# Loading each group's results at its own count of landed units, adding them two groups at a time on TensorE, and adding groups 0 and 1 on VectorE

## What is computed

```python
logits = jnp.einsum('bsd,de->bse', x, Wg)
P = jax.nn.softmax(logits, axis=-1)
_, topk_idx = jax.lax.top_k(P, K)                    # K = 2 of E = 8 experts
mask = jax.nn.one_hot(topk_idx, E, dtype=x.dtype).sum(-2)
P_norm = P * mask / ((P * mask).sum(axis=-1, keepdims=True) + EPS)
h = jax.nn.gelu(jnp.einsum('bsd,edf->ebsf', x, W1) + b1[:, None, None, :], approximate=False)
y_e = jnp.einsum('ebsf,efd->ebsd', h, W2) + b2[:, None, None, :]
g = _silu(jnp.einsum('ebsd,bse->bsd', y_e, P_norm))
x = x + s * g                                        # s: the second block's attention-like branch
```

## Time and profile before

| | |
|---|---|
| median of 3 runs | 446.04 us (444.91 to 446.62) |
| profiled execution: span from the first to the last instruction | 445.2 us |
| TensorE busy | 409.0 us, 92% of the span |
| VectorE busy | 284.5 us, 64% |
| ScalarE busy | 213.8 us, 48% |
| GpSimd busy | 155.7 us, 35% |

### The profile page before, as it was taken

One profiled execution on the slowest core, in us unless ns is written; L12 is line 12 of the kernel. 1 busy time (PEld: TensorE's weight loads), 2 busy tenths in 40 slices (PEclk: granted clock), 3 DMA queues, 4 the chain that ended last, 5 costly groups with the idle time before them and its releaser, 6 DMA issues. The chain is left out here.

```text
span 445.2 us, 9851 instructions
## 1 busy us (share of the span) xinstructions
PE 409.0 (92%) x2944; PEld 344.6 (77%) x2944; DVE 284.5 (64%) x1137; ACT 213.8 (48%) x525; POOL 155.7 (35%) x215
## 2 busy tenths in 40 slices
PE   7699989999999999999988999888999999999882
PEld 7579777878869779787767779777899999998630
DVE  4889889888887878878867657412233343433327
ACT  3364555565554545543424353333555555555412
POOL 6340015013233340443433011534454555455510
PEclk9999999999999999999999999999999999999998
DMA  7449411154064330131222223321222222222576
GB/s 181 123 114 166 57 40 42 50 170 135 13 192 122 81 79 25 47 83 53 75 54 61 66 51 80 101 80 54 68 71 67 78 71 71 61 77 68 169 275 193
DMA packets 64210, 40.80 MB, mean 92 GB/s; under 512 B 18340, under 2 KB 57128, under 8 KB 64168
## 3 DMA queue, kind: packets, MB, share of 16 engines
q1 hardware_dynamic: 59472, 31.27, 28.2%
q0 software_dynamic: 4352, 8.99, 6.1%
q10 hardware_dynamic: 344, 0.03, 0.1%
HBM read 21.78 MB, written 18.48 MB: 90 GB/s over the span
## 5 line engine op out<-in xcount | busy, mean ns | idle before, releaser
L694 POOL DMA_INDIRECT routed<-send,slot x64 | 64.5, 1008 | 129.1 <-DMA routed<-send,slot 57.5
L703 POOL DMA_INDIRECT results<-nat,y_to x72 | 69.8, 969 | 89.0 <-DVE nat L1638 65.4
L1029 PE MATMUL psA<-xuT,w_all 128*128 128x256 f32 x288 | 68.9, 381 | 3.5 <-ACT h1T L1239 3.2
L1239 ACT ACTIVATE h1T<-psA,b1T 128x256 f32<-128x256 f32 x144 | 63.1, 473 | 12.0 <-PE psB L1052 7.5
L1029 PEld LDWEIGHTS psA<-xuT,w_all 128*128 128x128 f32 x288 | 50.6, 190 | 11.5 <-issue 2.9
L1041 PE MATMUL psC<-w_all,h1T 128*128 128x128 f32 x464 | 56.7, 275 | 1.0 <-DVE nat L1622 1.0
L1610 DVE TENSOR_SCALAR xu<-ring 128x256 f32 (+1 forms) x38 | 11.2, 295 | 71.2 <-DMA ring<-routed 67.0
L1041 PEld LDWEIGHTS psC<-w_all,h1T 128*128 128x128 f32 x464 | 54.1, 192 | 1.3 <-ACT h1T L1239 1.1
L1230 ACT ACTIVATE xuT<-psB 128x256 f32<-128x256 f32 x37 | 14.2, 383 | 61.6 <-PE psB L1019 45.8
L843 PE MATMUL psB<-xnT,w_l 128*128 128x512 f32 x64 | 34.3, 618 | 0.0
L1170 ACT ACTIVATE hg0T<-psB,b1T 128x512 f32<-128x512 f32 x32 | 22.0, 688 | 22.9 <-PE psB L845 22.8
(11 more groups left out here) (289 smaller groups left out, 851.8 us busy)
## 6 DMA issues: line engine op xcount, KB each, us to landing
ring<-routed SPq DMA_DIRECT2D x38, 130.0 KB
inv<-inv_room SPq DMA_DIRECT2D x8, 512.0 KB
w_all<-results SPq DMA_DIRECT2D x15, 256.0 KB, 4.1
routed<-ring SPq DMA_DIRECT2D x24, 130.0 KB, 6.7
n_room<-nT SPq DMA_DIRECT2D x8, 256.0 KB
w_all<-in_L_ffn_W_dram SPq DMA_DIRECT2D x1, 2048.0 KB
out_dram<-x_all SPq DMA_DIRECT2D x8, 256.0 KB, 2.3
results<-nat,y_to POOLq DMA_INDIRECT x72
```

What stands on the lines that cost most here:

```text
L694: pool.indirect_dma_start(routed[:, :], bass.IndirectOffsetOnAxis(ap=slot[par][:, c, t:t + 1], axis=0), send[par][:, c, t, :], None).then_ ...
L703: pool.indirect_dma_start(results[:, :], bass.IndirectOffsetOnAxis(ap=y_to[:, par, a:a + 1], axis=0), yw[:, par, a, :], None).then_inc(S[f ...
L1029: last = mm(psA[:, j // 2, (j % 2) * UNIT:(j % 2 + 1) * UNIT], w1_all[:, e, j * P:(j + 1) * P], xuT[:, :], start=True, stop=True)
L1239: f(h1T[:, j, :], psA[:, j // 2, (j % 2) * UNIT:(j % 2 + 1) * UNIT], ACT.Gelu, bias=b1T[:, n:n + 1]).then_inc(S["gelu_ready"], 1)
```

## The change

Four things change together.

1. **Counts per group.** VectorE now keeps how far each expert's region was filled after each group (`filled` has a row for each group), and `make_table()` works out two counts for each group from it: the number of units that must have landed before the group's lower rows are whole (that of expert 6), and the same for its higher rows (that of expert 7). SP reads these counts from `table` (`units_due`) and waits for each before it loads that group's rows.
2. **When a landing is told.** POOL waits for the unit ahead, and raises `y_landed`, between a unit's two transfers instead of behind them, and once more at the end.
3. **The sums.** VectorE adds the rows of groups 0 and 1 itself, from SBUF; TensorE takes the others two groups at a time: lower, lower, higher, higher.
4. **The surplus unit.** When the count of units is odd, POOL sends one unit too many. VectorE's part in that (`surplus_results`) now stands behind `finish(1)`, and gives it row numbers outside of the results.

```diff
-            def load_results(c, to, signal):
-                for g in range(groups):
-                    at = c * tokens + g * GW
-                    sp.dma_start(to[g], results[at:at + GW, :].rearrange("(p t) d -> p t d", t=TILES)
-                                 ).then_inc(signal[g], 16)
-
+        DUE_AT = 2 * E + 2
+        def units_due(eng, g, part):
+            at = DUE_AT + 2 * g + part
+            return eng.value_load(table[0:1, at:at + 1], min_val=FIRST_ALL, max_val=MAX_UNITS)
...
+            def load_results(c, g, to, signal):
+                at = c * tokens + g * GW
+                sp.dma_start(to[g], results[at:at + GW, :].rearrange("(p t) d -> p t d", t=TILES)
+                             ).then_inc(signal[g], 16)
+
+            for g in range(groups - 2):
+                wait_on(sp, "y_landed", units_due(sp, g, 0))
+                load_results(0, g, res_lower, lower_in)
+            due = [units_due(sp, g, 1) for g in range(groups - 1)]
             wait_on(sp, "y_landed", bounds[E - 1])
-            load_results(0, res_lower, lower_in)
+            for g in range(groups - 2, groups):
+                load_results(0, g, res_lower, lower_in)
+            for g in range(groups - 1):
+                wait_on(sp, "y_landed", due[g])
+                load_results(1, g, res_higher, res_in)
             sp.wait_ge(all_landed, 1)
-            load_results(1, res_higher, res_in)
+            load_results(1, groups - 1, res_higher, res_in)
...
                 for a in range(HALVES):
+                    if a and not (isinstance(u, int) and u == 0):
+
+                        pool.wait_ge(S[f"y_sent{1 - par}"], (u + par) * (8 * HALVES))
+                        pool.sem_inc(S["y_landed"], 1)
                     pool.indirect_dma_start(
                         results[:, :], bass.IndirectOffsetOnAxis(ap=y_to[:, par, a:a + 1], axis=0),
                         yw[:, par, a, :], None).then_inc(S[f"y_sent{par}"], 16)
-                if not (isinstance(u, int) and u == 0):
-
-                    pool.wait_ge(S[f"y_sent{1 - par}"], (u + par) * (8 * HALVES))
-                    pool.sem_inc(S["y_landed"], 1)
...
             pool.wait_ge(S["y_sent1"], pairs_end * (8 * HALVES))
+            pool.sem_inc(S["y_landed"], 1)
             pool.sem_inc(all_landed, 1)
...
-            for g in range(groups):
-                pe.wait_ge(lower_in[g], 16)
-                if g == 0:
-                    wait_on(pe, "s1_ready", groups)
-                elif g == 4:
-                    pe.wait_ge(S["xuT_ready"], bounds[E] + 1)
-                elif g == 6:
-                    wait_on(pe, "yb_ready", bounds[E])
-                mm(sum_ps_of(g), ident[:, :], res_lower[g], start=True, stop=False)
-            for g in range(groups):
-                pe.wait_ge(res_in[g], 16)
-                mm(sum_ps_of(g), ident[:, :], res_higher[g], start=False, stop=True).then_inc(S["sum_ps"], 1)
+            for g0 in range(SUMS_BY_DVE, groups, 2):
+                for g in (g0, g0 + 1):
+                    pe.wait_ge(lower_in[g], 16)
+                    if g == 4:
+                        pe.wait_ge(S["xuT_ready"], bounds[E] + 1)
+                    elif g == 6:
+                        wait_on(pe, "yb_ready", bounds[E])
+                    mm(sum_ps_of(g), ident[:, :], res_lower[g], start=True, stop=False)
+                for g in (g0, g0 + 1):
+                    pe.wait_ge(res_in[g], 16)
+                    mm(sum_ps_of(g), ident[:, :], res_higher[g], start=False, stop=True).then_inc(S["sum_ps"], 1)
...
-                f(th1[g % 2][:, :, :], tiles(sum_ps_of(g)), ACT.Silu).then_inc(S["silu1_ready"], 1)
+                f(th1[g % 2][:, :, :], res_lower[g] if g < SUMS_BY_DVE else tiles(sum_ps_of(g)), ACT.Silu).then_inc(S["silu1_ready"], 1)
...
+                late = slice(E - 2, E)
+                link(v.tensor_tensor(due_f[:, :, :], filled[0:1, 1:, late],
+                                     region0[0:1, late].unsqueeze(1).broadcast_to([1, groups, 2]), ALU.subtract))
+                link(v.tensor_scalar(due_i[:, :, :], due_f[:, :, :], float(UNIT - 1), None, ALU.add))
+                link(v.tensor_scalar(due_i[:, :, :], due_i[:, :, :], UNIT.bit_length() - 1, None,
+                                     ALU.logical_shift_right))
+                link(v.tensor_scalar(due_f[:, :, :], due_i[:, :, :], float(FIRST_UNITS), -float(FIRST_UNITS), ALU.max,
+                                     ALU.add))
+                v.tensor_tensor(table[:, DUE_AT:].rearrange("p (g c) -> p g c", c=2), due_f[:, :, :],
+                                bound_f[:, late].unsqueeze(1).broadcast_to([1, groups, 2]), ALU.add)
...
-            wait_on(dve, "yw_ready", bounds[E])
-            dve.sem_inc(S["yw_ready"], 1)
-
+            def surplus_results():
+
+                wait_on(dve, "yw_ready", bounds[E])
+                dve.sem_inc(apart, 1)
+                wait_on(dve, "y_landed", bounds[E] - 1)
+                v.tensor_scalar(y_to[:, bass.ds(bounds[E] % 2, 1), :].rearrange("p r a -> p (r a)").unsqueeze(2),
+                                fill[:, 0, :, COL_ID:COL_ID + 1].bitcast(I32), 0.0, None,
+                                ALU.add).then_inc(S["yw_ready"], 1)
...
             dve.wait_ge(S["s1_ready"], groups)
+            for g in range(SUMS_BY_DVE):
+                dve.wait_ge(lower_in[g], 16)
+                dve.wait_ge(res_in[g], 16)
+                v.tensor_tensor(res_lower[g], res_lower[g], res_higher[g], ALU.add).then_inc(S["sum_sb"], 1)
             for g in range(groups):
                 finish(g)
+                if g == 1:
+                    surplus_results()
```

More of the change, by code:

```diff
@@ L74 @@
 FIRST_X = 2
+SUMS_BY_DVE = 2
 ROOTS_TO = {0: 1, 1: 3, 3: 8}
@@ L267, in two_block_kernel @@
         slot = [sb(f"slot_{i}", [P, CHOICES, TILES], U32) for i in range(2)]
-        filled = sb("filled", [P, E])
+        filled = sb("filled", [P, groups + 1, E])
         send = [sb(f"send{i}", [P, CHOICES, TILES, ROW]) for i in range(2)]
@@ L273, in two_block_kernel @@
         bound_f = sb("bound_f", [1, E + 1])
-        table = sb("table", [1, 2 * E + 2], I32)
+        table = sb("table", [1, 2 * E + 2 + 2 * groups], I32)
+        due_f = sb("due_f", [1, groups, 2])
+        due_i = sb("due_i", [1, groups, 2], I32)
         kT = sb("kT", [P, GW])
@@ L386, in two_block_kernel @@
             "y_landed",
-            "sum_ps", "mix_ready", "silu1_ready", "x2_ready", "x_out",
+            "sum_ps", "sum_sb", "mix_ready", "silu1_ready", "x2_ready", "x_out",
         )}
@@ L1263, in _ @@
             for g in range(groups):
-                act.wait_ge(S["sum_ps"], g + 1)
+                if g < SUMS_BY_DVE:
+                    act.wait_ge(S["sum_sb"], g + 1)
+                else:
+                    act.wait_ge(S["sum_ps"], g + 1 - SUMS_BY_DVE)
                 if g >= 2:
                     act.wait_ge(S["mix_ready"], g - 1)
-                f(th1[g % 2][:, :, :], tiles(sum_ps_of(g)), ACT.Silu).then_inc(S["silu1_ready"], 1)
+                f(th1[g % 2][:, :, :], res_lower[g] if g < SUMS_BY_DVE else tiles(sum_ps_of(g)), ACT.Silu).then_inc(S["silu1_ready"], 1)
         @block.vector
@@ L1298, in weight_products @@
                 dve.sem_inc(S["yw_ready"], SEEDED["yw_ready"])
-                v.tensor_copy(filled[:, :], region0[:, :]).then_inc(prep_dve, 1)
+                v.tensor_copy(filled[:, 0, :], region0[:, :]).then_inc(prep_dve, 1)
                 dve.wait_ge(prep_dve, 3)
@@ L1537, in work @@
                                          rank_ps[:, 0:TILES * E].rearrange("p (t e) -> p t e", e=E),
-                                         filled[:, :].unsqueeze(1).broadcast_to([P, TILES, E]), ALU.add))
-                    v.tensor_tensor(filled[:, :], filled[:, :], rank_ps[:, TILES * E:],
+                                         filled[:, g:g + 1, :].broadcast_to([P, TILES, E]), ALU.add))
+                    v.tensor_tensor(filled[:, g + 1, :], filled[:, g, :], rank_ps[:, TILES * E:],
                                     ALU.add).then_inc(S["rank_read"], 1)
@@ L1545, in work @@
                     if g == groups - 2:
-                        link(v.scalar_tensor_tensor(filled[:, :], region0[:, :], float(FIRST_UNITS * UNIT),
-                                                    filled[:, :], ALU.add, ALU.max))
+                        link(v.scalar_tensor_tensor(filled[:, g + 1, :], region0[:, :], float(FIRST_UNITS * UNIT),
+                                                    filled[:, g + 1, :], ALU.add, ALU.max))
                     if g == groups - 1:
@@ L1589, in make_table @@
             def make_table():
-                link(v.tensor_tensor(cnt_f[:, :], filled[0:1, :], region0[0:1, :], ALU.subtract))
+                link(v.tensor_tensor(cnt_f[:, :], filled[0:1, groups, :], region0[0:1, :], ALU.subtract))
                 link(v.tensor_scalar(cnt_i[:, :], cnt_f[:, :], float(UNIT - 1), None, ALU.add))
@@ L1603, in make_table @@
```

(4 more changed lines are left out.)

## The result

| | before | changed |
|---|---|---|
| median | 445.76 us (4 runs, 444.91 to 446.62) | 451.97 us (4 runs, 451.08 to 452.21) |
| ratio | 1 | 1.0134, 95% interval 1.0109 to 1.016 |
| span of the profiled execution | 445.2 us | 450.0 us |

The change makes the kernel 1.34% slower by the ratio of its runs; the medians differ by 6.2 us, and the forecast was a median of 451.2. Run again later, where the kernel before took 449.86 us, the same two kernels gave 1.0103 (1.0068 to 1.0138).

A forecast was written before the change was run, and what follows sets the result against it. The end was taken as bound by when group 0's higher rows arrive, then VectorE's 10.7 us. TensorE's path +3.0 and clock 1.7 gave +4.7, table +0.5: +5.2, a median of 451.2 us, range 447.5 to 455.0.

The forecast's parts named there:

- SP's reads: End of kernel, SP: thirteen reads of `table`, 0.6 us each, 1.1 with a load, put higher 0 at 428.9, before 427.09.
- Landings: End of kernel, loads: run starts with lower 6 at 427.9; higher 0 lands at 432.3, higher 1 at 433.2, higher 2 at 434.0.
- TensorE's order, +0.6: End of kernel, TensorE: ten products in a row after higher 2, 8.6 us, put VectorE's end at 445.5, +3.0.
- VectorE's own +2.4: End of kernel, VectorE alone: `finish(0)` 2.1 us later plus 0.3 for `surplus_results`; hidden under TensorE's +3.0.
- The clock, +1.7: End of kernel: TensorE idle 9 us, clock at 1.2 GHz, first two products at half pace, 1.7 us more.
- The surplus unit, 0.3: End of kernel, VectorE: `surplus_results`, one small operation of 0.17 and some register work, put at 0.3 us.
- The table, +0.5: `make_table`, ahead of its signal: five more dependent steps, some 1.0 us, less 0.5 of slack; 0.5 us late.
- POOL, 0: POOL's moved wait and earlier count: worth nothing, as SP issues higher 0 at 428.9 anyway; up to 1.2 were SP free.
- the clock stays up: Rival, TensorE at the end: clock stays up or comes back sooner, +3.0 + 0.5, 449.5 us; chance 0.12.
- the reads overlap one another: Rival, SP at the end: reads overlap one another and the loads, kernel gets faster, 443.5 us; chance 0.08.
- no change within 0.5%: Rival, whole kernel: reads of 0.5 us, a warm clock and a hidden table give 448 us; chance 0.09.
- The clock comes back late: Rival, TensorE at the end: four products at half pace cost 3.4, not 1.7, 453 us; all ten 458; chance 0.15.

The follow-up runs named there:

- the best kernel: Changed kernel with SP's thirteen reads moved ahead of the looped units and all lower products before the higher ones on TensorE: 445.68 us against 448.87, ratio 0.9938.

## Why the prediction was right

The time (451.2 for 451.97) and its sign came out, and the chain that was forecast, from SP's reads to the late higher rows, the slow clock and VectorE's waits, is in the profile; some sizes were off. Step by step, times counted from the last `ring` load being in:

- **SP's reads.** Forecast: higher 0 issued 11.9 us on. Measured: 11.2. A read in a row took 0.55 us, not 0.6 (the seven reads from 421.4 to 424.7), and a pair 1.02, not 1.1. The Trainium skill's floor of about 600 ns for one `tensor_load` ("DMA: Bandwidth & Descriptors", Latency and other measured facts) lies a little above what this trace shows, 0.55, and a little below the 0.64 of the earlier trace rows. That the reads cost by themselves is shown (1.0063).
- **Landings.** Higher 2 took 5.6 us from its issue, and higher 0 was added from 430.97 on, 4.7 us behind its issue, where 3.4 was forecast from a run on idle DMA engines. Ahead of it stood lower 6 and 7, as the forecast had it; they had landed at 427.9 and 428.6. Why higher 0 came over 2 us behind lower 7, and not 0.82, isn't shown. So TensorE resumed 17.9 us on, not 17.05. In the two other profiles of this order it was 16.7 and 17.1.
- **TensorE's order, +0.6 over VectorE's own +2.4.** Right in kind: ten products in a row, VectorE waiting from group 4 on (2.37 us; 0.29 already at group 3). With the lower products first the tail was 27.9, 2.5 over before: VectorE's own path, as forecast. That this kernel's measured ratio is only 1.0013 shows how far one profile's tail can be from the mean of the runs.
- **The clock, +1.7.** This is the term that was mis-sized for the profiled execution: 3.1 measured, since the clock came back after 6.1 us of work at half pace, not 3.4. But the other two profiles show 2.1 and 1.5, so 1.7 is inside what the kernel does. The reason given, idleness of 9 us before the higher rows, was only partly right: the clock had fallen before, at 421.9, behind 3.4 us of idleness ahead of the first lower product, which the prediction didn't see, and the four lower passes did not bring it back.
- **The surplus unit, 0.3 on VectorE's path.** Its one operation, at 435.53, sets the next step back by 0.07 us (434.92 to 435.60, against 0.61 between such steps elsewhere). So the fourth part of the change costs next to nothing.
- **The table, +0.5.** TensorE's next products behind the table start at 277.33, 0.5 later than in the earlier trace rows, as forecast, and the unit's output is 0.5 late at 282. But all of this stands 0.35 earlier in that execution (the eight steps start at 272.78, for 273.13 before), so the five steps really cost some 0.9, and the slack of 0.5 wasn't there. By the first looped `ring` load, which is 1.3 us earlier than before (304.45 for 305.78), nothing of it is to be seen.
- **POOL, 0.** Right in this kernel, for the reason given (1.0097 with the move undone, 1.0103 and 1.0134 with it in: no gain from it). In the loop of the units POOL does wait for landings now, which the prediction ruled out (15 waits, 19.6 us, from 320 to 410, none before), but TensorE is busy for all of these 90 us in both kernels, so it costs nothing there. It was wrong in what it said would hold were SP free: not a gain of up to 1.2 us but a loss of 0.6% in the kernel before.
- **The sum** was +4.7 for the tail; the three profiles of this order with late reads have +6.9, +4.7 and +4.5. In the first, landings and clock put the tail 2.2 over the forecast, and the early end of the units, which no term foresaw, took 2.0 off again: that its span, 450.0, is so near to the 450.4 forecast for it is luck. The other two profiles bear the sum out. The difference of the medians, 5.2 by the forecast, was 6.2 the first time and 4.2 the second.

Of the rivals, that the clock stays up fell, that the reads overlap one another fell too (thirteen starts, 0.55 to 1.02 us apart), and so did no change within 0.5%. *The clock comes back late* was nearly what the first profile shows (3.1 of its 3.4 us), and the second lies between it and the forecast (2.1). What stays open: what brings the wait of 1.87 us at 306, why the units end anywhere from 414.9 to 423.5 in these profiles (415.0 and 417.9 in the changed kernel's two), and whether the best kernel gains from POOL's wait being put back.

## What to carry to other kernels

Count what an engine's queue must do between its last wait and the load that everything waits for: a run-time count that is read there costs 0.55 us or more, and thirteen of them more than the earlier start that they were to bring. Read such values where the queue has time, and look at what then stands behind them. Put all work that needs only the early operand ahead of the first wait for the late one: it stands in idle time there, and if the clock has fallen, that work can bring it back before the work on the critical path begins, as in the kernel with lower products first. A wait that is put between two transfers of one unit holds the second one back for as long as the landing ahead takes in the traffic of that moment (3.4 to 5.7 us here), not for the 2.24 of a quieter one.

## What the runs showed of the hardware

- The granted clock fell to the level of 1.2 GHz (0.50) after 3.4 us of idleness and 0.6 us of work in the changed kernel (at 421.9), after 2.2 us of idleness in that with lower products first (421.8) and after 2.3 in the kernel before with POOL's moved wait (432.2); through 2.7 us of idleness in the kernel with early reads and POOL's wait back (425.6 to 428.3) it stayed at 1.00. It came back after 6.1 and 4.1 us of work at half pace in the changed kernel's two profiles, 2.8 in that with POOL's wait back and 5.7 in that with lower products first. The Trainium skill's account ("TensorE: Matmul & The Clock Gate", Part 1: half by default, released by sustained work) agrees with that in kind.
- An indirect transfer of 128 rows landed 2.24 us after its issue in the kernel before (424.79), where the DMA engines' share was 0.97 at its issue and 0.46 and 0.25 in the next 2 us. It took 3.39 us in the changed kernel (418.87), 3.88 and 4.52 with POOL's moved wait alone (419.04, 423.70) and 4.26 and 5.7 with early reads (419.19, 424.23), all beside loads of 256 KB.
- Reads of a register from SBUF on SP don't overlap one another: thirteen start 0.55 us apart in a row, and 1.02 with a DMA issue between them. The read itself takes 0.27 us, its register and assert instructions 0.15 and 0.02; what fills the rest isn't shown.
